# Four-layer sequence block: another order in the head of a first-phase step, two table calls on ScalarE, and the residual sum moved from GpSimd to VectorE

## The chip, the cores and the metric

One core of one Trainium2 chip runs the whole program in one launch. The metric is the device time of that launch in microseconds, of which lower is better. All data are float32 unless a line says otherwise.

## The reference

Four blocks run in sequence on x of 4 sequences, 1024 rows, 128 features. After each one, x becomes layernorm(x + block(x)).

- **Block 1, mixer and MLP.** `u = rmsnorm(x)`; `u @ in_proj` gives z (256 wide), xBC (512 wide) and 4 step sizes. xBC goes through a causal depthwise convolution of 4 taps with bias and then silu; the step sizes go through softplus. A state scan over the rows (4 heads of 64, 128 states) gives y, which is gated with silu(z), normalised, and projected back to 128; the result is added to x and called x1 below. Then `h = rmsnorm(x1)` and `mlp = (silu(h @ gate) * (h @ up)) @ down` with a hidden width of 512. The block returns x1 + mlp.
- **Block 2, expert layer.** 8 experts, a softmax gate, the best 2 of them weighted and summed.
- **Block 3, attention.** Layernorm, 16 heads of 8, full softmax over 1024 keys with a relative position bias, and an output projection.
- **Block 4, routed experts.** 8 experts of capacity 512, the best 2, with gather and scatter.

The change lies in block 1 and in what runs beside it. The residual sum x + x1, to which mlp is added before the layernorm, is one of its items.

## The kernel before

The kernel has three phases: a first phase (blocks 1 and 2 and the inputs of attention), attention, and the routed experts with the output. Every engine has its own program, written out by hand as a sequence of instructions, and the engines meet only through semaphores. An instruction waits in order, so whatever is queued behind a waiting instruction on its engine waits too.

**The first phase is software-pipelined over the four sequences.** The list `SLOTS` has six steps (m, p, q): m is the sequence whose mixer runs, p the one whose MLP and expert layer run, q the one whose attention inputs are made. Steps 1, 2 and 3 have an m and a p, steps 2 to 4 a p and a q; step 0 has only m = 0, step 5 only q = 3. Each step has a **head** and then a loop over 8 chunks of 128 rows. In the profiled execution the heads of steps 1, 2 and 3 begin near 121, 253 and 409 us, step 4 near 558 us, and attention near 664 us.

**The head.** For m: the step sizes (`step_sizes`), 12 input projections (`project`, one 128x128 weight by 512 rows each, in two passes), of which 4 are z and 8 go through the convolution. ScalarE copies each projection out of PSUM (`evac_projection`) and, for a convolved tile, makes the first tap with the bias (`tap`). VectorE adds the other three taps (`convolve`, L1782, three instructions of 128x512). ScalarE applies silu (`silu_conv`). For p: `rms_apply` (L1859) scales x1 by its inverse root into `x1n`, TensorE turns it (`rows_turned_mlp`), ScalarE copies it to `xnT` (`evac_T`, L1091). Then come eight steps n of the MLP: TensorE multiplies with `w_gate` and `w_up`, ScalarE makes silu of the first (`gate_silu`, L1179), VectorE multiplies both into `hidT` (`hidden`, L1867). After that TensorE runs `down` for the two halves of the rows, and VectorE adds each half to the residual sum `xa` (`skip_sum`, L1872). For q: `expert_norm` normalises a half of block 2's sum (L1699) and takes its statistics (L1681, L1686), and `tail_norm` applies attention's own layernorm (L1699).

**What ties the MLP's steps together.** The matmuls rotate through PSUM banks 5, 6 and 7, so on TensorE the gate product of step n waits for the product on VectorE of step n - 2:

```python
                if n >= 2:
                    pe.wait_ge(S.hid_ready, 2 * HID_TILES * b + n - 1)
                mm(bank(mlp_bank(2 * n)), tile(w_gate, f), xnT[:, half(H)])
```

TensorE's order in the loop is gate n, up n, projection 4 + n of the next mixer. `down` for half H waits for 7 + H products of `hidden`. VectorE's order before the change is `step_sizes`, convolution 0, both `rms_apply`, convolution 1, both halves of `expert_norm`, convolutions 2 and 3, and only then `hidden` 0.

**GpSimd** computes inverse roots (L1422), the two products `aU` of the first chunks (L1451), and, in the head, the residual sum `xa = xin + x1` (`skip_rows`, L1473). SyncE loads the input tile of sequence p + 2 after that sum (`res_sum`), and the stores of attention rows (`store_rows`) are queued behind that load.

ScalarE's function tables are loaded where the program changes between Exp and Silu. Copy, Identity and Square run with either of them. The load stands as ACT_TABLE_LOAD in the trace and carries the line of the activation that follows it.

Of the kernel before, what the change touches and what calls it, by code (L numbers as in the profile page):

```python
# [19 lines left out]
ALU = mybir.AluOpType  # L20
# [89 lines left out]
def build(nc, t):  # L110

    with ExitStack() as ctx:  # L112
        def sb(name, shape, dt=F32):
            return ctx.enter_context(nc.sbuf_tensor(name, shape, dt))
# [119 lines left out]
        rstd_mix = sb("rstd_mix", [P, NT])  # L234
        ss = sb("ss", [P, NT])
        rstd3 = sb("rstd3", [P, NT])

        o_rec = sb("o_rec", [P, HT, QUAD])
        smax = sb("smax", [P, 2, 16])
# [820 lines left out]
        def _(act):  # L1060
# [24 lines left out]
            def evac_T(kind, b, banks, **affine):  # L1085

                xnT_free(kind, b)
                for H in range(2):
                    act.wait_ge(S.xT_psum, turned(kind, b) + H + 1)
                    func = ACT.Identity if affine else ACT.Copy  # L1090
                    nc.scalar.activation(xnT[:, half(H)], bank(banks[H]), func, **affine).then_inc(S.xnT_ready, 1)  # L1091
# [18 lines left out]
            def evac_input(b):  # L1110
# [3 lines left out]
                for H, at in enumerate((TRB, SEGB)):  # L1114
                    act.wait_ge(S.in_T_psum, 2 * b + H + 1)
                    nc.scalar.activation(xinT[:, half(H)], bank(at), ACT.Copy).then_inc(S.in_T, 1)

            def step_exp(b):
                act.wait_ge(S.dt_abs, b + 1)
                nc.scalar.activation(dtu[:], dts[:], ACT.Exp, scale=-1.0).then_inc(S.dt_u, 1)  # L1120
# [94 lines left out]
            for m, p, q in SLOTS:  # L1215
                if m is not None:
                    evac_input(m)
                    step_exp(m)
                if p is not None:
                    mixed_squares(p, 1)  # L1220
                if m is not None:
                    for i in range(4):
                        evac_projection(m, i)
                        tap(m, i)
                if p is not None:
                    evac_T("mlp", p, (5, 6))
                for n in range(2 * HID_TILES):
                    if p is not None:
                        gate_silu(p, n)
                    if m is not None:  # L1230
                        evac_projection(m, 4 + n)
                        if 4 + n in CONVOLVED:
                            tap(m, CONVOLVED.index(4 + n))
                        if n >= 1:
                            silu_conv(m, n - 1)
                if m is not None:
                    silu_conv(m, N_CONV - 1)
                    decays(m)
                    chunk_copy(m, 0)
                if q is not None:  # L1240
                    act.wait_ge(S.w_late, LATE_LOADED)
                    act.wait_ge(S.late_ready, N_LATE)
                    evac_T("tail", q, (7, 6), scale=ln_g[:], bias=ln_b[:])
                if m is not None:
                    chunk_exp(m, 0, 0)
                    chunk_exp(m, 0, 1)
                if q is not None:
                    evac_queries(q)
                if m == 0:
                    act.wait_ge(S.w_late, LATE_LOADED)  # L1250
                    nc.scalar.activation(pick_rows[:].rearrange("k e n -> k (e n)"), pick_in, ACT.Copy).then_inc(S.late_ready, 1)
                for c in range(NT):
                    if m is not None and c < NT - 1:
                        chunk_copy(m, c + 1)
                        chunk_exp(m, c + 1, 0)
                    if p is not None and c == HT:
                        evac_gates(p)
                    if m is not None and c < NT - 1:
                        chunk_exp(m, c + 1, 1)
                    if m is not None and c in (2, 4, 6):  # L1260
                        gated_squares(m, c // 2 - 1)
                    if p is not None and c == 0:
                        evac_T("moe", p, (7, 5))
                    if p is not None and c == 2:
                        route_exp(p)
                    if q is not None and c < 3:
                        cut_part(q, c)
                    if m is not None and m + 1 < B and c == HT + 1:
                        input_squares(m + 1)
                if m is not None:  # L1270
                    gated_squares(m, HT - 1)
                    mixed_squares(m, 0)
# [104 lines left out]
        def _(pool):  # L1377
# [87 lines left out]
                                decay[:, 1, c].unsqueeze(2).to_broadcast([P, SSM_HEADS, SSM_DIM]),  # L1465
                                ALU.mult).then_inc(S.hdec_ready, 1)

            def skip_rows(b):

                pool.wait_ge(S.x1_ready, 2 * b + 2)  # L1470
                if b >= 1:
                    pool.wait_ge(S.normed, 6 * b - 4)
                g.tensor_tensor(xa[:], xin[:, b % 2], x1[:], ALU.add).then_inc(S.res_sum, 1)  # L1473

            input_root(0)
            g.memset(x3_all[:], 0.0).then_inc(S.zero_rows, 1)
            for m, p, q in SLOTS:
# [11 lines left out]
                    for H in range(2):  # L1489
                        norm_root(2, 6 * q + 4 + H, H)  # L1490
                if p is not None:
                    skip_rows(p)
                    for H in range(2):
                        norm_root(0, 6 * p + H, H)
                if m is not None:
# [126 lines left out]
        def _(dve):  # L1622
# [238 lines left out]
            def hidden(b, n):  # L1861
# [4 lines left out]
                    dve.wait_ge(S.q_part, 3 * (b - 1))  # L1866
                v.tensor_tensor(hidT[:, f, half(H)], silu_g[:, n % 2], bank(mlp_bank(2 * n + 1)), ALU.mult).then_inc(S.hid_ready, 1)  # L1867

            def skip_sum(b, H):
                dve.wait_ge(S.res_sum, b + 1)  # L1870
                dve.wait_ge(S.down_psum, 2 * b + H + 1)
                v.tensor_tensor(xa[:, own(H), :], xa[:, own(H), :], tiles4(5 + H), ALU.add).then_inc(S.skip_sum, 1)  # L1872
                dve.wait_ge(S.skip_sum, 2 * b + H + 1)
                statistics(xa, H, 0)
# [42 lines left out]
            def tail_norm(b, H):  # L1917
                if b >= 1:
                    dve.wait_ge(S.xT_psum, 2 * TURN_NO["tail", b - 1] + 2)
                normalise(kept(b), xn, H, 2, 6 * b + 4 + H)  # L1920
# [33 lines left out]
            for m, p, q in SLOTS:  # L1954
                if m is not None:
                    step_sizes(m)
                    convolve(m, 0)
                if p is not None:
                    for H in range(2):
                        rms_apply(p, H)  # L1960
                if m is not None:
                    convolve(m, 1)
                if q is not None:
                    for H in range(2):
                        expert_norm(q, H)
                if m is not None:
                    convolve(m, 2)
                for n in range(2 * HID_TILES):
                    if m is not None and n in (0, 3, 4, 5, 6):
                        convolve(m, 3 if n == 0 else n + 1)  # L1970
                    if p is not None:
                        hidden(p, n)
                    if q is not None and n == 2:
                        for H in range(2):
                            tail_norm(q, H)
                if p is not None:
                    for H in range(2):
                        skip_sum(p, H)
# [301 lines left out]
```

## Time and profile before

| what | value |
|---|---|
| median of 3 runs | 1643.79 us (1634.2, 1643.79, 1643.9) |
| the profiled execution | 1639.0 us, span 1637.3 us |
| mean granted TensorE clock | 0.904 |
| TensorE busy | 1378.8 us, 84% of the span |
| VectorE busy | 1116.4 us, 68% |
| ScalarE busy | 852.5 us, 52% |
| GpSimd busy | 314.6 us, 19% |

The span runs from the first to the last instruction. A granted clock of 1.00 is 2.4 GHz and 0.50 is 1.2 GHz. Busy shares are means over phases with different limits; attention alone is 876 us. In the rows below PE is TensorE's matmuls, DVE is VectorE, ACT is ScalarE and POOL is GpSimd, and L numbers are lines of the kernel.

### The profile page before, as it was taken

The numbers are of one execution on the slowest core, as the hardware profiler recorded it, in microseconds if no ns is written. First come the engines' busy times: TensorE is split into PE (matmuls) and PEld (weight loads), VectorE is DVE, ScalarE is ACT, GpSimd is POOL, SyncE is SP. The second block draws the span as 40 slices with busy tenths as digits, with TensorE's granted clock in tenths as the row PEclk, the third lists the DMA queues.
The fourth block names the chain that finished last, engine by engine and source line by source line (L and its number), as shares of the span: only waits on it lengthen the run. The fifth ranks groups of instructions, "written<-read, shape, count | busy, mean of one in ns | idle before, by whom it ended". The sixth has DMA issues, their size and how long they took to land. (4 is left out here: it accounts for less than half of the span.)

```text
span 1637.3 us, 20851 instructions
## 1 busy us (share of the span) xinstructions
PE 1378.8 (84%) x7344; PEld 615.8 (38%) x7344; DVE 1116.4 (68%) x2089; ACT 852.5 (52%) x1656; POOL 314.6 (19%) x444
## 2 busy tenths in 40 slices
PE   4778797889788877799999999999999999983560
PEld 2454473557355655122222333223332233322240
DVE  5647658565856555878888888888888888833115
ACT  5226214421532230277777777777777777772125
POOL 3221313122221301000000020141103211043351
PEclk9779998979889887589999999999999999996795
DMA  3070000020011247301111001111001100000224
GB/s 113 2 174 14 1 1 13 5 90 1 1 50 45 27 52 172 128 1 21 21 20 21 17 22 21 21 46 38 14 8 31 31 1 2 2 6 24 58 83 154
DMA packets 45965, 63.53 MB, mean 39 GB/s; under 512 B 8706, under 2 KB 33869, under 8 KB 44022
## 3 DMA queue, kind: packets, MB, share of 16 engines
q1 hardware_dynamic: 42790, 57.97, 14.6%
q0 software_dynamic: 3072, 4.23, 0.8%
q8 instruction: 59, 0.97, 0.3%
q14 instruction: 44, 0.36, 0.1%
HBM read 33.07 MB, written 31.15 MB: 39 GB/s over the span
## 5 line engine op out<-in xcount | busy, mean ns | idle before, releaser
L578 PE MATMUL ps<-space 128*32 128x512 f32 (+5 forms) x4608 | 860.3, 480 | 31.9 <-DVE smax L2048 7.6
L2048 DVE TENSOR_REDUCE smax<-ps 128x1 f32<-128x1024 f32 x512 | 605.2, 1220 | 116.1 <-PE ps L578 109.9
L1322 ACT ACTIVATE space<-ps 128x512 f32<-128x512 f32 x1024 | 555.5, 595 | 231.8 <-PE ps L578 231.1
L578 PEld LDWEIGHTS ps<-space 128*32 128x32 f32 (+5 forms) x4608 | 254.4, 110 | 614.2 <-ACT space L1322 329.2
L1420 POOL TENSOR_SCALAR eps_sum<-mv 128x4 f32<-128x4 f32 x32 | 7.3, 229 | 640.9 <-DVEq L1688 640.5
L578 PE MATMUL ps<-w_exp,space 128*128 128x128 f32 x512 | 86.2, 323 | 0.0
L1782 DVE SCALAR_TENSOR_TENSOR space<-space,conv_w 128x512 f32<-128x512 f32 x96 | 80.7, 850 | 4.2 <-ACT space L1151 1.6
L578 PEld LDWEIGHTS ps<-w_exp,space 128*128 128x128 f32 x512 | 74.1, 225 | 16.5 <-issue 16.5
L1198 ACT ACTIVATE btok<-ps 128x128 f32<-128x128 f32 x32 | 8.9, 277 | 135.1 <-DVE Gm L1800 68.8
L1530 POOL DMA_INDIRECT expert_in<-space,slot x64 | 62.9, 982 | 37.6 <-issue 19.3
L1902 DVE TENSOR_TENSOR space<-xnT,ps 128x512 f32<-128x512 f32 x64 | 42.1, 683 | 31.0 <-PE ps L578 31.0
L1204 ACT ACTIVATE space<-ps 128x512 f32<-128x512 f32 x64 | 38.1, 595 | 43.9 <-PE ps L578 43.8
L578 PE MATMUL ps<-space,w_in 128*128 128x512 f32 x96 | 54.7, 675 | 5.4 <-ACT space L1137 3.5
L571 PE MATMUL ps<-ident,space 128*128 128x128 f32 x192 | 32.6, 305 | 31.6 <-DVE space L1859 12.3
L578 PE MATMUL ps<-aU,ones 128*128 128x512 f32 x64 | 39.2, 697 | 22.9 <-ACT space L1204 22.6
L2203 DVE TENSOR_TENSOR space<-space,ps 96x512 f32<-96x512 f32 x16 | 10.9, 684 | 68.8 <-ACT space L1350 68.8
L578 PE MATMUL ps<-xnT,w_gate 128*128 128x512 f32 x64 | 39.5, 704 | 12.8 <-DVE space L1867 12.6
L1819 DVE TENSOR_TENSOR space<-space 128x512 f32<-128x512 f32 x32 | 28.7, 897 | 24.8 <-ACT space L1204 24.8
L1451 POOL TENSOR_TENSOR aU<-upto,av 128x512 f32<-128x512 f32 x32 | 36.9, 1157 | 41.4 <-PE ps L578 29.0
L1422 POOL TENSOR_TENSOR rstd<-eps_sum,neg_half 128x4 f32<-128x4 f32 x40 | 42.1, 1052 | 3.3
L1460 POOL TENSOR_TENSOR space<-space,decay 128x256 f32<-128x256 f32 x28 | 17.1, 612 | 120.5 <-issue 83.7
L571 PEld LDWEIGHTS ps<-ident,space 128*128 128x128 f32 x192 | 26.5, 158 | 36.3 <-issue 32.6
(246 smaller groups left out, 1457.3 us busy)
## 6 DMA issues: line engine op xcount, KB each, us to landing
q_rows<-space SPq DMA_DIRECT2D x24, 256.0 KB, 2.5
k_rows<-space SPq DMA_DIRECT2D x24, 256.0 KB, 2.8
space<-k_rows SPq DMA_DIRECT2D x16, 384.0 KB, 5.2
space<-q_rows SPq DMA_DIRECT2D x16, 384.0 KB, 6.8
expert_out<-x_all SPq DMA_DIRECT2D x2, 2048.0 KB, 20.4
space<-expert_out SPq DMA_DIRECT2D x4, 1024.0 KB, 8.8
v_rows<-space SPq DMA_DIRECT2D x4, 668.0 KB, 3.6
space<-v_rows SPq DMA_DIRECT2D x4, 668.0 KB, 6.5
```

The costliest lines, as they stand in the source:

```text
L571: last = nc.tensor.transpose(tile(dst, i), src(i), ident[:])
L578: return nc.tensor.matmul(out, lhsT, rhs, start=first, stop=last)
L1204: nc.scalar.activation(EL[:, c % 2, k].rearrange("p h n -> p (h n)"), bank(SEGB), ACT.Exp).then_inc(S.l_ready, 1)
L1322: nc.scalar.activation(prob[:, QUAD * (step % PROB_SETS) + unit % QUAD, :], bank(STB + unit % 2), ACT.Exp)\
L1422: g.tensor_tensor(out, eps_sum[:, 0:n], neg_half[:, 0:n], ALU.pow).then_inc(done, 1)
L1451: g.tensor_tensor(aU[:, c % 2], upto[:].unsqueeze(1).to_broadcast([P, SSM_HEADS, P]), av[:, c].unsqueeze(2).to_broadcast([P, SSM_HEADS, P] ...
L1460: g.tensor_tensor(xw[:, c % 2], xdt[:, c % 2], decay[:, 0, c].unsqueeze(2).to_broadcast([P, SSM_HEADS, SSM_DIM]), ALU.mult).then_inc(S.xw_ ...
L1530: g.indirect_dma_start(expert_in, bass.IndirectOffsetOnAxis(ap=slot[:, k, i:i + 1], axis=0), xrow[:, i, k, :], None, bounds_check=E * CAPA ...
L1782: ins = v.scalar_tensor_tensor(out, raw[:, f, lo + k:lo + k + HALF], conv_w[:, f, k:k + 1], out, ALU.mult, ALU.add)
L1819: v.tensor_tensor(Cs[:, c % 2], xbc[:, 3, c * P:(c + 1) * P].unsqueeze(1).to_broadcast([P, SSM_HEADS, P]), EL[:, c % 2, 1], ALU.mult).then ...
L1902: v.tensor_tensor(xs[:, k % XS_SLOTS], xnT[:, half(H)], bank(6 + k % 2), ALU.mult).then_inc(S.xs_ready, 1)
L2048: v.tensor_reduce(smax[:, N % 2, i:i + 1], ps[:, b0:b0 + 2, :].rearrange("p k n -> p (k n)"), AX.X, ALU.max).then_inc(S.s_max, 1)
```

## The change

- VectorE: both `rms_apply` come directly behind `step_sizes`; convolutions 0 and 1 follow. Convolutions 2 to 7 come one behind each of `hidden` 1 to 6. Where p and q both exist, the second half of `expert_norm` comes behind `hidden` 0, and `tail_norm` moves from behind step n = 2 to behind step n = 4.
- ScalarE: taps 2 and 3 come behind `evac_T`. A one-column Silu (`table_of`) stands ahead of `evac_T` where there is a p, and a one-column Exp behind the last `silu_conv` in every step.
- `skip_rows` leaves GpSimd and is done on VectorE behind the eighth `hidden`.

TensorE's and SyncE's programs are not edited.

```diff
@@ sb allocations
+        warm = sb("warm", [P, 2])
@@ ScalarE
+            def table_of(func, i):
+
+                nc.scalar.activation(warm[:, i:i + 1], neg_half[:, 0:1], func)
...
                 if m is not None:
-                    for i in range(4):
+                    for i in range(2):
                         evac_projection(m, i)
                         tap(m, i)
+                    for i in range(2, 4):
+                        evac_projection(m, i)
                 if p is not None:
+                    table_of(ACT.Silu, 0)
                     evac_T("mlp", p, (5, 6))
+                if m is not None:
+                    for i in range(2, 4):
+                        tap(m, i)
...
                 if m is not None:
                     silu_conv(m, N_CONV - 1)
+                table_of(ACT.Exp, 1)
+                if m is not None:
                     decays(m)
@@ GpSimd
-            def skip_rows(b):
-
-                pool.wait_ge(S.x1_ready, 2 * b + 2)
-                if b >= 1:
-                    pool.wait_ge(S.normed, 6 * b - 4)
-                g.tensor_tensor(xa[:], xin[:, b % 2], x1[:], ALU.add).then_inc(S.res_sum, 1)
...
-                    skip_rows(p)
@@ VectorE
+            def skip_rows(b):
+
+                if b >= 1:
+                    dve.wait_ge(S.normed, 6 * b - 4)
+                mine.wait(mine.n)
+                v.tensor_tensor(xa[:], xin[:, b % 2], x1[:], ALU.add).then_inc(S.res_sum, 1)
...
                 if m is not None:
                     step_sizes(m)
-                    convolve(m, 0)
                 if p is not None:
                     for H in range(2):
                         rms_apply(p, H)
                 if m is not None:
+                    convolve(m, 0)
                     convolve(m, 1)
                 if q is not None:
-                    for H in range(2):
-                        expert_norm(q, H)
-                if m is not None:
-                    convolve(m, 2)
+                    expert_norm(q, 0)
+                    if p is None:
+                        expert_norm(q, 1)
                 for n in range(2 * HID_TILES):
-                    if m is not None and n in (0, 3, 4, 5, 6):
-                        convolve(m, 3 if n == 0 else n + 1)
                     if p is not None:
                         hidden(p, n)
-                    if q is not None and n == 2:
+                    if q is not None and p is not None and n == 0:
+                        expert_norm(q, 1)
+                    if m is not None and 1 <= n <= N_CONV - 2:
+                        convolve(m, n + 1)
+                    if q is not None and n == 4:
                         for H in range(2):
                             tail_norm(q, H)
+                if p is not None:
+                    skip_rows(p)
                 if p is not None:
                     for H in range(2):
                         skip_sum(p, H)
```

## Rows read from the trace of the kernel before

**Rows 1.** Timeline of PE, step 2: start us, us, engine, line, what [idle before <-releaser].

```profile
263.72 1.91 PE L578 MATMUL ps<-xnT,w_gate 128*128 128x512 f32 x2 [0.19 <-ACT xnT L1091]
...
277.60 2.08 PE L578 MATMUL ps<-xnT,w_gate 128*128 128x512 f32 x2 [6.77 <-DVE space L1867]
...
295.59 7.38 PE L578 MATMUL ps<-w_down,space 128*128 128x128 f32 x64
```

**Rows 2.** Timeline of DVE, step 2.

```profile
257.99 3.63 DVE L1782 SCALAR_TENSOR_TENSOR space<-space,conv_w 128x512 f32<-128x512 f32 x3
261.54 1.28 DVE L1859 TENSOR_TENSOR space<-x,rstd 128x512 f32<-128x512 f32 x2
...
264.98 1.11 DVE L1699 TENSOR_SCALAR x_all<-x,mv,rstd 128x128 f32<-128x128 f32 x4
...
270.21 6.74 DVE L1782 SCALAR_TENSOR_TENSOR space<-space,conv_w 128x512 f32<-128x512 f32 x6
276.87 1.28 DVE L1867 TENSOR_TENSOR space<-space,ps 128x512 f32<-128x512 f32 x2
...
281.97 2.14 DVE L1699 TENSOR_SCALAR xn<-x_all,mv,rstd 128x128 f32<-128x128 f32 x8
284.02 2.32 DVE L1782 SCALAR_TENSOR_TENSOR space<-space,conv_w 128x512 f32<-128x512 f32 x3
286.26 0.68 DVE L1867 TENSOR_TENSOR space<-space,ps 128x512 f32<-128x512 f32 x1
286.86 2.32 DVE L1782 SCALAR_TENSOR_TENSOR space<-space,conv_w 128x512 f32<-128x512 f32 x3
...
299.50 0.69 DVE L1872 TENSOR_TENSOR xa<-xa,ps 128x512 f32<-128x512 f32 x1 [3.46 <-PE ps L578]
```

**Rows 3.** Timeline of POOL, step 2.

```profile
258.21 2.86 POOL L1451 TENSOR_TENSOR aU<-upto,av 128x512 f32<-128x512 f32 x2 [1.19 <-DVE av L1772]
...
271.83 2.33 POOL L1473 TENSOR_TENSOR xa<-xin,x 128x1024 f32<-128x1024 f32 x1
```

**Rows 4.** Timeline of ACT, step 2.

```profile
260.33 0.81 ACT L1151 ACTIVATE space<-space,conv_b,conv_w 128x512 f32<-128x512 f32 x1
...
264.19 1.28 ACT L1179 ACT_TABLE_LOAD   x1
265.67 0.60 ACT L1179 ACTIVATE space<-ps 128x512 f32<-128x512 f32 x1 [0.20 <-PE ps L578]
```

**Rows 5.** Windows of step 2: us, PE, PEld, DVE, ACT, POOL busy, PEclk, DMA, GB/s.

```profile
277.60:281.10 3.50, 3.50 (x5) 1.52 (x6) 0.55 (x1) 0.60 (x1) 0.00 (x0) 0.51 0.01 4
281.10:295.60 14.50, 14.42 (x34) 5.68 (x32) 13.95 (x26) 11.42 (x20) 0.00 (x0) 1.00 0.00 1
```

**Rows 6.** Timelines of ACT, PE and DVE, step 1.

```profile
128.07 0.81 ACT L1151 ACTIVATE space<-space,conv_b,conv_w 128x512 f32<-128x512 f32 x1
...
134.03 2.07 PE L578 MATMUL ps<-xnT,w_gate 128*128 128x512 f32 x2
...
140.47 0.69 DVE L1867 TENSOR_TENSOR space<-space,ps 128x512 f32<-128x512 f32 x1 [0.46 <-PE ps L578]
...
156.88 7.38 PE L578 MATMUL ps<-w_down,space 128*128 128x128 f32 x64
```

**Rows 7.** Timelines of DVE and PE, step 3.

```profile
413.69 3.64 DVE L1782 SCALAR_TENSOR_TENSOR space<-space,conv_w 128x512 f32<-128x512 f32 x3
...
451.56 7.38 PE L578 MATMUL ps<-w_down,space 128*128 128x128 f32 x64
```

**Rows 8.** Timeline of DVE, step 4.

```profile
569.35 0.69 DVE L1867 TENSOR_TENSOR space<-space,ps 128x512 f32<-128x512 f32 x1 [0.77 <-PE ps L578]
```

**Rows 9.** Timelines of PE behind the heads of steps 2 and 3.

```profile
308.16 1.97 PE L578 MATMUL ps<-aU,ones 128*128 128x512 f32 x2 [1.94 <-ACT space L1204]
...
464.13 1.12 PE L578 MATMUL ps<-aU,ones 128*128 128x512 f32 x2 [1.94 <-ACT space L1204]
```

**Rows 10.** Window of the attention phase.

```profile
664.00:1540.00 876.00, 814.39 (x4473) 246.73 (x4474) 675.23 (x918) 589.66 (x1087) 127.17 (x200) 0.95 0.10 23
```

## The prediction

> **What bounds the kernel now.** I read the page first: TensorE is busy 84% of the span, and about half of that is attention, which the change does not touch [rows 10]. So the change has to be read from the heads. I read the timelines of TensorE, VectorE, ScalarE and GpSimd over the head of step 2, then laid those of steps 1, 3 and 4 beside them.
>
> In step 2 TensorE begins the first gate product at 263.72, and its third gate product waits 6.77 us, until 277.60, for a product of VectorE [rows 1]. The releaser is `hidden` 0. Its two PSUM operands had been there for some ten us: VectorE did not reach it before 276.87, because two halves of `expert_norm` (264.98 to 270.21) and convolutions 2 and 3 stand ahead of it, and these last two were slowed [rows 2]. The wait costs twice, since TensorE comes back at half clock: 0.51 in the stretch after it, 1.00 in the one behind [rows 5], and the gate product's two passes take 2.08 us [rows 1], while 34 passes, 17 products, take 14.42 us at full clock [rows 5], 0.85 each. Later in the loop VectorE goes at 2.84 us a step (284.02 to 286.86: a convolution of 2.24 and a `hidden` of 0.60 by their starts [rows 2]) while TensorE has three products a step, 2.55 us. From there to `down` at 295.59 both keep nearly the same pace. What is to be seen is that VectorE has work for the whole head and does it in an order in which TensorE runs dry once. The limit after a reordering is VectorE's own sum of work.
>
> **The parts.** All sums are made against the profiled execution, 1639.0 us (span 1637.3, 1.7 around it), which is 4.8 under the median of the runs; these differ by 9.7 us among themselves.
>
> *VectorE's order, step 2.* VectorE is free at 257.99. Up to the end of `hidden` 6 the new order has: both scalings 1.2 (two in 1.28 [rows 2]), seven convolutions x 2.24 = 15.7, both halves of `expert_norm` 5.2 (264.98 to 270.21), `tail_norm` 2.05 (281.97 to 284.02), seven `hidden` x 0.60 = 4.2. Added to it is 1.3 us of blocking by GpSimd's two `aU` products: three instructions took 3.63 instead of 2.32 beside them [rows 2, 3]. The products do not go away, so I keep the 1.3, wherever it lands. What goes is the second blocking: six convolution instructions took 6.74 instead of 4.6 while `skip_rows` ran for 2.33 [rows 2, 3]. The sum is 29.7 us, `hidden` 6 ends at 287.7, and `down` can begin there at about 287.8 instead of 295.59 [rows 1]: 7.7 us gained, if VectorE is never kept waiting. `hidden` 7 ends 2.84 later, at 290.5, and the second half of `down` needs it only 3.7 us after the start of the first (7.38 for both).
>
> *Is VectorE kept waiting?* Its arrival at `hidden` 0 is 257.99 + 1.2 + 1.3 + 2 x 2.24 + 2.6 = 267.6. The first up product ends at most 3.8 us after the first gate starts (two of 1.91 at half clock [rows 1]), 265.6 if the gate starts at 261.8. It is not. Gate 2 needs `hidden` 0 (268.2) and TensorE has the six products of the first two steps done 7.2 us after the first gate (3.8 and four of 0.85), at 269.0: the 6.77 us wait is gone.
>
> *The start of the gate products.* `rms_apply` ends about 260.3 instead of 262.8, and ScalarE drops two taps of 0.8 ahead of the copy: tap 3 ended at 261.1 [rows 4], so the projections are copied by 259.5. Then the Silu load, 1.28, and the one-column call. No such call is in the trace; it lies between nothing and the 0.60 of the 128x512 activation [rows 4], and I take 0.2 because one column is nearer to nothing. With the copy of 0.6 the gate starts at about 261.7, against 263.72 [rows 1]. Taps 2 and 3 then run under the first gate product and are needed by VectorE only at 271.
>
> *What the Silu call is worth.* Before, the load ran under the first gate product: it ended at 265.47, and silu still waited 0.20 for TensorE [rows 4]. So the early call saves nothing there, and stands instead ahead of a copy on the path to TensorE; in steps 2 and 3 VectorE arrives later anyway and hides it. I cost it at nothing. The Trainium skill (ScalarE: Activation LUTs, What ACT_TABLE_LOAD costs) gives a switch 2.66 us in all, the load of 1.28 and a drain of 1.38. Here the load started directly behind the copy before it and its activation directly behind it where TensorE was done, which leaves no room for a drain. By the Trainium skill the first gate of step 1 would come 1.4 us later, and the sum below would be smaller by that.
>
> *Step 3* has the same rows: 413.69 + 29.7 + 0.1 = 443.5 against 451.56 [rows 7], 8.1 us gained.
>
> *Step 1* has no q, so TensorE bounds its start. Tap 3 ended at 128.9 [rows 6]; less 1.6, plus 1.28, 0.2 and 0.6, the gate starts at 129.5 instead of 134.03, 4.5 earlier. `hidden` 1 was bound by TensorE, 6.44 behind the gate (140.47 against 134.03 [rows 6]), so it ends at 136.5. Then VectorE has five convolutions and five `hidden` to the end of `hidden` 6, 5 x 2.84 = 14.2: 150.8. `down` starts at 151.0 instead of 156.88 [rows 6], 5.9 gained.
>
> *Step 4* has no m. `hidden` 1 started at 569.35 [rows 8], and now comes behind half an `expert_norm`; the gate product that needs it was due at 570.8 and would wait until 571. I take 0.3 lost, between 0 and 0.6; `tail_norm` only moves two steps on. The Exp call there saves a load that stood ahead of work for which VectorE was not waiting: nothing.
>
> *`skip_rows` on VectorE.* 1.3 us (two halves of 128x512 took 1.28 [rows 2]). It is queued ahead of `skip_sum`, which waited 3.46 us for `down` in step 2 [rows 2]. As `hidden` 7 now ends 2.8 behind `hidden` 6, not 0.6, the cover shrinks to about 291.7 - 290.5 = 1.2 us: just hidden, bounds 0 to 0.3. Without the cover it costs 1.3 a step. SyncE's input load waits for this sum, some 18 us later than now, and the stores queued behind it are due only in the chunk loop; the input tile is read about 80 us later. Nothing.
>
> *TensorE's clock.* This is the term that the trace does not fix. With `tail_norm` between steps 4 and 5 TensorE runs dry for 2.3 us ahead of its last three products. If the clock falls there they take twice 0.85 each: 2.6 more, of which some 2.2 reach `down`. Before, the same product of `aU` behind the same idle of 1.94 us took 1.97 us in step 2 and 1.12 in step 3 [rows 9]: such a gap brings half clock in one case of two. I take half, 1.1 in each of steps 2 and 3; the bounds are 0 and, with `down` beginning at half clock too, 3.9. The Trainium skill (TensorE: Matmul & The Clock Gate, Part 1) advises to leave the ramp out as under 1% of a typical span. Its term is 2.2 us here; without it the forecast would be 1618. The rows after the wait show that it has a price at this size [rows 5].
>
> **Sum:** 5.9 + 7.7 + 8.1 - 0.3 - 2.2 = 19.2 us. 1639.0 - 19.2 = 1619.8, so 1620. Everything behind `down` (decay sums, chunk loop, attention) hangs on it through TensorE and moves with it.
>
> **Rivals.**
>
> *A smaller gain.* VectorE is fully packed, so each hand-off that arrives late adds up, and the clock falls in every head. Price: 3.9 in steps 2 and 3, a half-clock `down` of 1.7 in step 1, 1.3 for an uncovered `skip_rows` in three steps: 7.8 + 1.7 + 3.9 = 13.4, of which 2.2 are in my sum. Gain 8.0, time 1631. For it: the cover of 1.2 is thin. Against: VectorE had 13.95 of 14.50 us busy before [rows 5] without losing its pace.
>
> *No change.* The head ends earlier and the time is given back behind it, in a wait that does not move (a transfer, a root on GpSimd). Time 1639. Against: `down` follows TensorE's own products with no idle row, and `skip_sum` waits for nothing but TensorE. For: attention is 876 us at clock 0.95 [rows 10], and 0.02 of clock there would be 18 us, as large as the gain.
>
> *Slower: the clock stays at half through the MLP loop.* In the new loop TensorE stops for a moment in each step instead of once for long. If that keeps the clock at 1.2 GHz, the 24 products of a loop take 24 x 1.7 = 41 us from the first gate: `down` at 302.7 in step 2 (7.1 later than before), 6.7 later in step 3, 13.6 in step 1. Sum +27, time 1666. It decides from a mean of 1.4 us a product on (295.59 - 261.7 = 33.9 for 24). Against: TensorE worked 2.55 of 2.84 us a step before, at 1.00 [rows 5], and that pace stays.
>
> *The calls do nothing.* If the load is not placed at the call, the gate starts 1.5 earlier, silu later, and VectorE's sum still decides: within 1 us of the forecast and part of it.
>
> **Numbers.** Forecast 0.69 (gains from 12 to 24), smaller gain 0.15, no change 0.10, slower 0.06. With the clock term at its lower bound and step 1 at full clock the gain is 21.4 + 1.8 = 23, 1616; with the upper one it is 13, 1626; the runs stand from 4.8 below to 4.9 above the profiled one. The range is 1611 to 1634, which leaves out the last two rivals and a little of the first. A change below 1% (16.4 us, to 1627.4) could not be told from none. The forecast lies above that with nine parts in ten, and the smaller gain with three: 0.69 x 0.93 + 0.15 x 0.3 = 0.69 faster; slower 0.06; the same 0.25.
>
> **What would show it.** Right: no idle of several us at the third gate of steps 2 and 3; `down` there about 30 us behind the end of `step_sizes` instead of 37.7; VectorE without a gap from the scalings to `hidden` 7; no convolution instruction of 2.9 us; the first gate of step 1 some 4.5 us earlier in its head. Wrong: VectorE waiting for TensorE in the loop, TensorE at 0.50 over the loop, `skip_sum` starting behind `skip_rows` by more than 0.3, or attention longer by more than a few us.

## The result and the profile after

The kernel after takes 1612.56 us where the kernel before takes 1639.31. The head of each step is shorter, and attention starts earlier by about as much.

| | before | after |
|---|---|---|
| median of 4 runs each | 1639.31 us | 1612.56 us (1609.37 to 1617.73) |
| ratio, 95% interval | | 0.9852 [0.9822, 0.9883] |
| span of the profiled execution | 1637.3 us | 1612.9 us |
| start of `av` (last of `step_sizes`) to start of `down`, steps 1, 2, 3 | 31.27, 37.71, 37.98 us | 24.71, 30.35, 30.77 us |
| start of the first scaling of x1 to start of `down`, step 4 | 19.70 us | 19.82 us |
| attention begins at | 664.07 us | 639.73 us |

A ratio here is the kernel's time by that of the kernel before, run beside it, with a 95% interval. This one is a gain of 24 us, or 19 to 29 by its interval. Of the 24.3 us by which attention starts earlier in the profile, the heads give 6.56 + 7.36 + 7.21 - 0.12 = 21.0; the other 3.3 lie outside the heads. Attention itself is as long as before, at the same clock [rows 10] (us, then busy us and instructions of PE, PEld, DVE, ACT and POOL, granted clock, DMA share, GB/s):

```profile
639.00:1516.00 877.00, 814.99 (x4474) 247.05 (x4475) 675.74 (x920) 589.82 (x1087) 127.58 (x200) 0.95 0.10 24
```

VectorE in step 2 after the change, from the end of `step_sizes` to both `skip_sum`, answers to [rows 2]:

```profile
253.33 0.19 DVE L1777 TENSOR_TENSOR av<-dt,a_neg 128x32 f32<-128x32 f32 x1
253.44 2.13 DVE L1864 TENSOR_TENSOR space<-x,rstd 128x512 f32<-128x512 f32 x2
255.49 5.33 DVE L1787 SCALAR_TENSOR_TENSOR space<-space,conv_w 128x512 f32<-128x512 f32 x6
260.74 1.11 DVE L1704 TENSOR_SCALAR x_all<-x,mv,rstd 128x128 f32<-128x128 f32 x4
...
263.38 0.69 DVE L1872 TENSOR_TENSOR space<-space,ps 128x512 f32<-128x512 f32 x1 [0.21 <-DVE mv L1691]
263.99 1.11 DVE L1704 TENSOR_SCALAR x_all<-x,mv,rstd 128x128 f32<-128x128 f32 x4
...
266.63 0.69 DVE L1872 TENSOR_TENSOR space<-space,ps 128x512 f32<-128x512 f32 x1 [0.21 <-DVE mv L1691]
267.24 2.32 DVE L1787 SCALAR_TENSOR_TENSOR space<-space,conv_w 128x512 f32<-128x512 f32 x3
...
277.97 2.14 DVE L1704 TENSOR_SCALAR xn<-x_all,mv,rstd 128x128 f32<-128x128 f32 x8
280.02 0.68 DVE L1872 TENSOR_TENSOR space<-space,ps 128x512 f32<-128x512 f32 x1
280.62 2.32 DVE L1787 SCALAR_TENSOR_TENSOR space<-space,conv_w 128x512 f32<-128x512 f32 x3
282.86 0.68 DVE L1872 TENSOR_TENSOR space<-space,ps 128x512 f32<-128x512 f32 x1
283.46 2.32 DVE L1787 SCALAR_TENSOR_TENSOR space<-space,conv_w 128x512 f32<-128x512 f32 x3
285.69 0.68 DVE L1872 TENSOR_TENSOR space<-space,ps 128x512 f32<-128x512 f32 x1
286.29 1.22 DVE L1879 TENSOR_TENSOR xa<-xin,x 128x1024 f32<-128x1024 f32 x1
287.60 0.69 DVE L1884 TENSOR_TENSOR xa<-xa,ps 128x512 f32<-128x512 f32 x1
```

From 253.44 to the end of `hidden` 6 at 283.54 VectorE stands still twice, for 0.21 us each time. Every convolution inside the MLP loop takes 2.32. The two scalings took 2.13 instead of 1.28, and the six convolution instructions behind them 5.33 instead of 4.56 (what six take in sum_only, undisturbed): that is the blocking by `aU`, 1.6 us in all, which has moved with GpSimd's row:

```profile
253.66 2.80 POOL L1464 TENSOR_TENSOR aU<-upto,av 128x512 f32<-128x512 f32 x2 [1.18 <-DVE av L1777]
```

`skip_rows` is the row of 1.22, and `skip_sum` follows it at once. TensorE beside it, against [rows 1]:

```profile
255.62 0.66 PE L572 MATMUL ps<-ident,space 128*128 128x128 f32 x4 [0.77 <-DVE space L1864]
257.00 1.12 PE L579 MATMUL ps<-xnT,w_gate 128*128 128x512 f32 x2 [0.72 <-ACT xnT L1092]
257.97 1.02 PE L579 MATMUL ps<-xnT,w_up 128*128 128x512 f32 x2
...
264.13 1.12 PE L579 MATMUL ps<-xnT,w_gate 128*128 128x512 f32 x2 [1.71 <-DVE space L1872]
...
267.37 1.12 PE L579 MATMUL ps<-xnT,w_gate 128*128 128x512 f32 x2 [0.41 <-DVE space L1872]
...
280.76 1.13 PE L579 MATMUL ps<-xnT,w_gate 128*128 128x512 f32 x2 [2.04 <-DVE space L1872]
281.72 1.02 PE L579 MATMUL ps<-xnT,w_up 128*128 128x512 f32 x2
282.58 1.02 PE L579 MATMUL ps<-space,w_in 128*128 128x512 f32 x2
283.68 7.38 PE L579 MATMUL ps<-w_down,space 128*128 128x128 f32 x64
```

The wait of 6.77 us at the third gate is 1.71 now. The gap behind `tail_norm` is there, 2.04, and no gate product takes 1.9 or more. The windows with these two gaps, and the stretch behind the second, were granted full clock throughout:

```profile
262.20:264.10 1.90, 0.22 (x1) 0.00 (x0) 1.65 (x9) 1.11 (x2) 0.70 (x2) 1.00 0.00 0
278.50:280.80 2.30, 0.26 (x2) 0.04 (x1) 2.30 (x9) 1.12 (x2) 0.00 (x0) 1.00 0.00 0
281.10:283.60 2.50, 2.50 (x6) 0.76 (x4) 2.43 (x5) 0.60 (x1) 0.00 (x0) 1.00 0.00 0
```

In step 1 GpSimd's `skip_rows` used to run beside the scalings of x1, 129.03 to 131.56, and VectorE in the kernel before needed 3.42 us for the two:

```profile
129.28 3.42 DVE L1859 TENSOR_TENSOR space<-x,rstd 128x512 f32<-128x512 f32 x2
```

Now they end sooner, and TensorE begins the first gate, against 134.03 [rows 6], at:

```profile
130.57 1.12 PE L579 MATMUL ps<-xnT,w_gate 128*128 128x512 f32 x2 [1.04 <-ACT xnT L1092]
```

From there to `down` (window, columns as above) it has no idle moment, 20.70 of 20.70 us busy, and VectorE has:

```profile
130.60:151.30 20.70, 20.70 (x49) 9.22 (x50) 19.28 (x29) 16.35 (x28) 0.00 (x0) 1.00 0.00 1
```

`skip_sum` of step 1 on VectorE waits 0.70 us for the end of `down`'s first half:

```profile
155.12 0.69 DVE L1884 TENSOR_TENSOR xa<-xa,ps 128x512 f32<-128x512 f32 x1 [0.70 <-PE ps L579]
```

### The profile page after: what moved, and what is told of

It is laid out like the page before. It is cut to its first block and busy times, and to the rows that moved or that the text cites. A ratio compares the mean times of both kernels' runs of the same rounds, so it can differ in the third digit from the quotient of the medians.

```text
span 1612.9 us, 20861 instructions
## 1 busy us (share of the span) xinstructions
PE 1368.9 (85%) x7344; PEld 610.7 (38%) x7344; DVE 1114.2 (69%) x2093; ACT 854.0 (53%) x1666; POOL 304.9 (19%) x440
## 5 line engine op out<-in xcount | busy, mean ns | idle before, releaser
L579 PE MATMUL ps<-w_exp,space 128*128 128x128 f32 x512 | 82.7, 314 | 0.0
L1787 DVE SCALAR_TENSOR_TENSOR space<-space,conv_w 128x512 f32<-128x512 f32 x96 | 74.8, 788 | 2.3
L1535 POOL DMA_INDIRECT expert_in<-space,slot x64 | 63.0, 984 | 37.6 <-issue 19.3
L579 PE MATMUL ps<-aU,ones 128*128 128x512 f32 x64 | 39.2, 697 | 22.9 <-ACT space L1209 22.8
L572 PE MATMUL ps<-ident,space 128*128 128x128 f32 x192 | 31.3, 293 | 20.7 <-DVE space L1754 11.2
L579 PE MATMUL ps<-xnT,w_gate 128*128 128x512 f32 x64 | 35.3, 634 | 12.1 <-DVE space L1872 9.4
L1802 DVE TENSOR_TENSOR space<-ps,dt 128x256 f32<-128x256 f32 x32 | 13.4, 420 | 38.9 <-PE ps L579 38.1
```

The lines of the kernel that those rows point to most:

```text
L572: last = nc.tensor.transpose(tile(dst, i), src(i), ident[:])
L579: return nc.tensor.matmul(out, lhsT, rhs, start=first, stop=last)
L1535: g.indirect_dma_start(expert_in, bass.IndirectOffsetOnAxis(ap=slot[:, k, i:i + 1], axis=0), xrow[:, i, k, :], None, bounds_check=E * CAPA ...
L1787: ins = v.scalar_tensor_tensor(out, raw[:, f, lo + k:lo + k + HALF], conv_w[:, f, k:k + 1], out, ALU.mult, ALU.add)
```

## Experiments

Times of steps below are from `av` to `down` unless said otherwise. The first four kernels ran on a chip on which the kernel before takes 1673.53 us, the others on chips where it takes 1638.67 and 1637.52, so whole times are compared within a group only. Single profiles of one kernel agree within 0.4 us in the heads of steps 1 to 3, but differ by some us outside them (after_again shows it).

**order_only.** The kernel before, with nothing but VectorE's new order (the hunks of the change for it, `skip_rows` left on GpSimd):

```diff
-                    convolve(m, 0)
                 if p is not None:
                     for H in range(2):
                         rms_apply(p, H)
                 if m is not None:
+                    convolve(m, 0)
                     convolve(m, 1)
...
+                    if q is not None and p is not None and n == 0:
+                        expert_norm(q, 1)
+                    if m is not None and 1 <= n <= N_CONV - 2:
+                        convolve(m, n + 1)
-                    if q is not None and n == 2:
+                    if q is not None and n == 4:
```

> Only VectorE's new order; the residual sum stays on GpSimd, ScalarE is as before. Theory 1 (the new order removes the 6.8 us wait of the third gate product, and VectorE's own work then sets the start of down): from the end of the step sizes to down, steps 2 and 3 take about 32.4 us (30.3 of the changed kernel and 2.1 for a convolution blocked by the sum on GpSimd) instead of 37.7 and 38.0, step 1 26.8 instead of 31.3; gain 15 us, 1624. Rival (the gain is the end of the blocking by GpSimd): steps 2 and 3 stay near 36 us, gain under 6.

Measured: 25.67, 32.38 and 32.42 us, and 1661.3 us, ratio 0.9921 [0.9895, 0.9947], 13 us. The order gives 5.6, 5.3 and 5.6 a step. What is missing against the full change in steps 2 and 3 (2.0 and 1.7) shows in one row of VectorE, the first convolution in the loop of step 2:

```profile
268.03 4.34 DVE L1782 SCALAR_TENSOR_TENSOR space<-space,conv_w 128x512 f32<-128x512 f32 x3
```

and in the one of GpSimd beside it:

```profile
268.68 2.35 POOL L1473 TENSOR_TENSOR xa<-xin,x 128x1024 f32<-128x1024 f32 x1
```

The same three instructions take 2.32 where `skip_rows` does not run: VectorE lost 2.02 us to an instruction of 2.35 us that began beside them. TensorE then stands idle in the loop for 2.10 us in step 2 and 2.08 in step 3, and in both the clock falls: at the gate product in step 3, at the up product behind it in step 2.

```profile
273.11 1.10 PE L578 MATMUL ps<-xnT,w_gate 128*128 128x512 f32 x2 [2.10 <-DVE space L1867]
274.05 1.79 PE L578 MATMUL ps<-xnT,w_up 128*128 128x512 f32 x2
...
420.91 2.02 PE L578 MATMUL ps<-xnT,w_gate 128*128 128x512 f32 x2 [2.08 <-DVE space L1867]
```

On the blocking: the Trainium skill (SBUF — State Buffer, SBUF: two separate sides) has a port pair that VectorE with two SBUF inputs and GpSimd hold in turn, each for its whole instruction; the 2.02 of 2.35 us agree.

**sum_only.** The kernel before, with `skip_rows` on VectorE ahead of `skip_sum`:

```diff
...
@@ GpSimd
-                    skip_rows(p)
@@ VectorE
+                if p is not None:
+                    skip_rows(p)
                 if p is not None:
                     for H in range(2):
                         skip_sum(p, H)
```

> Only the residual sum on VectorE; order and ScalarE as before. Theory 1: VectorE reaches the first product 2.1 us sooner in steps 2 and 3, and the scaling of step 1 is 2.1 us sooner; each head gains 2, in all 6 us, 1633, and the wait at the third gate stays at 4.6 us. Rival (the blocking is the main cost): 12 us or more. Third possibility (the wait ends with something else): nothing.

Measured: 28.33, 36.13 and 36.11, that is 2.94, 1.58 and 1.87 us sooner, and ratio 0.9964 [0.994, 0.9988], 6 us. (Step 4 is 0.36 shorter too, but it is so in tables_only as well, which leaves this sum alone.) The removed blocking is worth what was expected in total: 6.4 us in the three heads. The wait at the third gate of step 2 shrinks from 6.77 by 2.18 us, and the product still takes 2.08 (TensorE):

```profile
275.77 2.08 PE L578 MATMUL ps<-xnT,w_gate 128*128 128x512 f32 x2 [4.59 <-DVE space L1859]
```

Both parts alone sum to 16.5 + 6.4 = 22.9 us in steps 1 to 3, against 21.1 in the full change. In steps 2 and 3 the parts add up (6.9 and 7.4 against 7.36 and 7.21); in step 1 they give 8.5 against 6.56, since TensorE bounds that step from its first gate on, and order_only alone already starts the gate as early (3.8 us behind `av`, against 4.0).

**tables_only.** The kernel before, with both table calls, and the taps where they were:

```diff
                 if p is not None:
+                    table_of(ACT.Silu, 0)
                     evac_T("mlp", p, (5, 6))
...
                     silu_conv(m, N_CONV - 1)
+                table_of(ACT.Exp, 1)
+                if m is not None:
```

> Only the two calls that load function tables ahead, everything else as before. Theory 1: no effect, within 1 us, as the load ran under the first gate product. Rival (each early load takes 1.28 us off a head): 4 to 5 us faster. If the load holds back the copy of xnT: up to 1.5 us slower per head, 4 us in all.

Measured: 30.38, 38.42, 37.54, and ratio 1.0007 [0.9981, 1.0032]. The calls do what they say: the load stands at the call. No gain is to be seen, and one of over 3 us is excluded by the interval, which rules out the rival of 4 to 5 us. ScalarE in step 2 of this kernel:

```profile
264.89 1.28 ACT L1121 ACT_TABLE_LOAD   x1
266.18 0.20 ACT L1121 ACTIVATE warm<-neg_half 128x1 f32<-128x1 f32 x1
266.79 1.25 ACT L1092 ACTIVATE xnT<-ps 128x512 f32<-128x512 f32 x2 [0.41 <-PE ps L572]
```

The load and the call end before the copy's operand is there, and the copy still waits 0.41 us.

**tail_late.** The kernel after, with `tail_norm` behind the eighth `hidden` in steps 2 and 3, so that no `hidden` waits for it:

```diff
-                    if q is not None and n == 4:
+                    if q is not None and n == (4 if m is None or p is None else 7):
```

> The changed kernel with tail_norm behind the eighth hidden in steps 2 and 3 instead of behind the fifth. Theory 1: VectorE's work ahead of down is 2.05 us shorter, down starts 2 us sooner in both steps, the second half of the residual sum is late by 0.5; gain 3 us on the changed kernel, about 1610. Rival (TensorE's own products bound the loop): down does not move, and the late skip_sum makes it 1 to 4 us slower.

Measured: 28.30 and 28.72 instead of 30.35 and 30.77, 2.05 sooner in both, exactly the length of `tail_norm`. The head is VectorE's sum. The first copy of the decay products of the first chunk (`Gm`), which also needs VectorE, gains only 1.4 (39.0 and 39.4 us behind `av`, against 40.4 and 40.8), because both `skip_sum` now come behind `tail_norm`. The full change did not run on this chip, so 1647.38 us (0.9833 [0.98, 0.9866]) ranks it only against the kernel before, and the 3 us expected over the change are not tested by whole times.

**after_again, conv_ahead, conv_first, late_nosilu** ran on one chip. The first is the full change once more.

> The changed kernel as it is, for comparison on one chip. From the end of the step sizes to down: 24.7, 30.4 and 30.8 us in steps 1, 2 and 3, as in its first profile, since VectorE's work sets them and not chance in the clock; 21 us of gain from the heads, and 0 to 4 us more or less outside them.

Measured: 24.39, 30.38, 30.78; 1617.57 us, ratio 0.9856 [0.9829, 0.9882]. The heads repeat within 0.03 in steps 2 and 3. What lies outside them does not. From `down` of step 1 to `av` of step 2 it is 104.7 here (granted clock 0.90) and 102.1 in the first profile (0.92), with the same instructions; the kernel before had 101.0 (0.93), but tables_only, with VectorE's old order and the old sum, 104.3, so the change is not shown to lengthen it. From `down` of step 3 to the scaling of step 4 it is 108.1 here, 105.2 in the first profile and 108.5 before. Step 4's own stretch is 20.24, not 19.82. Single profiles differ by some us outside the heads, and part of it goes with the clock that TensorE was granted there.

**conv_ahead.** Convolution n + 2 behind `hidden` n, one step sooner, so that all eight are ahead of `hidden` 6:

```diff
-                    if m is not None and 1 <= n <= N_CONV - 2:
-                        convolve(m, n + 1)
+                    if m is not None and n <= N_CONV - 3:
+                        convolve(m, n + 2)
```

> The changed kernel with each of convolutions 2 to 7 one step earlier, behind hidden 0 to 5, so that convolution 7 stands ahead of hidden 6. VectorE's total work is the same. Theory 1 (down starts when VectorE has done what is queued up to hidden 6): down 2.24 us later in each of steps 1 to 3, 6.7 us slower than the changed kernel. Rival (only the wait at the third gate counted): within 1 us of the changed kernel.

Measured: 25.25, 33.06, 32.93: 2.68 and 2.15 later in steps 2 and 3, but 0.86 in step 1; 1623.13 us, 5.6 more than after_again. So keeping the eighth convolution behind `hidden` 6 is one full term of the gain in steps 2 and 3; in step 2 a fall of the clock, the gate of 1.97 below, comes on top. Step 1 has slack on VectorE, since TensorE bounds it. The idle rows of TensorE's loop in step 2 of this kernel:

```profile
267.46 1.13 PE L579 MATMUL ps<-xnT,w_gate 128*128 128x512 f32 x2 [1.74 <-DVE space L1872]
272.88 1.97 PE L579 MATMUL ps<-xnT,w_gate 128*128 128x512 f32 x2 [2.57 <-DVE space L1872]
286.80 1.12 PE L579 MATMUL ps<-xnT,w_gate 128*128 128x512 f32 x2 [1.66 <-DVE space L1872]
```

**conv_first.** Convolution 0 again ahead of both `rms_apply`:

```diff
                     step_sizes(m)
+                    convolve(m, 0)
                 if p is not None:
                     for H in range(2):
                         rms_apply(p, H)
                 if m is not None:
-                    convolve(m, 0)
                     convolve(m, 1)
```

> The changed kernel with convolution 0 ahead of the scaling of x1, as before the change. Theory 1: in steps 2 and 3 down does not move, as VectorE has the same work up to it and arrives at hidden 0 later than TensorE; in step 1 the first gate is 2.3 us later and up to 1.4 of it reaches down. In all 1 to 2 us slower than the changed kernel. Rival (the early scaling is what gains): 2.3 us in each of three heads, 7 slower.

Measured: 26.51, 30.05, 30.87, against 24.39, 30.38, 30.78. The early gate is worth 2.1 us in step 1 and nothing in steps 2 and 3, as the sum of VectorE says, though step 1 lost 0.7 more than the bound. The medians differ by 6.5 us, more than the expected 1 to 2; the intervals (0.9873 to 0.9919 here) overlap, and what the heads do not show of it stays open. The gate stands behind a longer idle of TensorE here. In step 1 it takes 1.13 us behind an idle of 3.17, in step 2 2.07 behind one of 3.41:

```profile
131.32 1.17 PE L572 MATMUL ps<-ident,space 128*128 128x128 f32 x8 [3.17 <-DVE space L1864]
132.63 1.13 PE L579 MATMUL ps<-xnT,w_gate 128*128 128x512 f32 x2
...
261.88 1.21 PE L572 MATMUL ps<-ident,space 128*128 128x128 f32 x8 [3.41 <-issue]
263.27 2.07 PE L579 MATMUL ps<-xnT,w_gate 128*128 128x512 f32 x2 [0.18 <-ACT xnT L1092]
```

**late_nosilu.** tail_late, and no Silu call:

```diff
                 if p is not None:
-                    table_of(ACT.Silu, 0)
                     evac_T("mlp", p, (5, 6))
```

> tail_norm behind the eighth hidden in steps 2 and 3 (as in tail_late), and without the Silu call ahead of the copy of xnT; the load then stands under the first gate product as before. Theory 1: down at 28.3 and 28.7 us behind the step sizes in steps 2 and 3, as with the call; in step 1 the first gate 1.3 us sooner and down up to 0.9 sooner. 3 to 4 us faster than the changed kernel. Rival (the call is what starts the gates early): first gate later in every head, down of step 1 up to 1.3 us later.

Measured: 24.22, 28.32, 28.72; 1612.82 us, ratio 0.9847 [0.9824, 0.987], 4.8 below after_again with overlapping intervals. Against tail_late the heads of steps 2 and 3 are unchanged, so the Silu call is worth nothing there, neither way. In step 1 the load only changes its place: the gate starts 0.9 sooner (2.78 behind `av` instead of 3.69), and gives 0.17 to `down`, because the load now stands behind both taps and the second up product waits for it. Step 2 shows the same hand-off on TensorE:

```profile
254.72 1.02 PE L579 MATMUL ps<-xnT,w_gate 128*128 128x512 f32 x2
...
258.89 1.12 PE L579 MATMUL ps<-xnT,w_up 128*128 128x512 f32 x2 [0.56 <-ACT space L1184]
```

and on ScalarE, where the load follows the taps:

```profile
255.42 1.51 ACT L1156 ACTIVATE space<-space,conv_b,conv_w 128x512 f32<-128x512 f32 x2
256.94 1.28 ACT L1184 ACT_TABLE_LOAD   x1
258.24 0.60 ACT L1184 ACTIVATE space<-ps 128x512 f32<-128x512 f32 x1
```

**after_third, combined** ran on one chip. The first is the full change again; the second is late_nosilu with taps 2 and 3 behind the first silu of the MLP, and `skip_sum` cut in two so that the inputs of the first chunk are taken ahead of the statistics of the second half:

```diff
@@ ScalarE
-                if m is not None:
-                    for i in range(2, 4):
-                        tap(m, i)
...
+                    if m is not None and n == 0:
+                        for i in range(2, 4):
+                            tap(m, i)
@@ VectorE
+            def skip_statistics(b, H):
...
-                    for H in range(2):
-                        skip_sum(p, H)
+                    skip_sum(p, 0)
+                    skip_statistics(p, 0)
+                    skip_sum(p, 1)
                 if m is not None:
                     chunk_inputs(m, 0)
+                if p is not None:
+                    skip_statistics(p, 1)
```

> The changed kernel again, beside the version below on one chip. Heads of 24.7, 30.4 and 30.8 us from the step sizes to down within 0.4 us; outside the heads it may differ by several us from profile to profile.

> The changed kernel with tail_norm behind the eighth hidden in steps 2 and 3, no Silu call, taps 2 and 3 behind the first gate silu, and the statistics of the second half of the residual sum behind the first chunk's inputs. Theory 1: down 28.3 and 28.7 us behind the step sizes in steps 2 and 3, 23.5 in step 1, where TensorE is then without a gap from its first gate on; the first chunk's inputs come 0.7 to 1.3 us closer behind down. In all 5 to 7 us faster than the changed kernel. Rival (what is taken from the head comes back in the chunk loop, as the statistics and the norm are late there): within 1 us of the changed kernel although down starts sooner.

Measured, after_third: 24.40, 30.36, 30.77; 1619.75 us, 0.9886 [0.9852, 0.992]. Measured, combined: 23.70, 28.30, 28.72, and `Gm` 32.9, 37.6 and 38.0 us behind `av`, against 34.4, 40.4 and 40.8 in after_third; 1604.24 us, 0.9801 [0.9773, 0.9829]. It beats both kernels: its interval lies below that of after_third, which ran beside it. In its step 2 TensorE begins `down` at:

```profile
285.19 3.03 PE L579 MATMUL ps<-w_down,space 128*128 128x128 f32 x25
```

and VectorE does, from the second `skip_sum`:

```profile
293.32 0.69 DVE L1883 TENSOR_TENSOR xa<-xa,ps 128x512 f32<-128x512 f32 x1 [0.21 <-DVE mv L1690]
294.13 0.42 DVE L1801 TENSOR_TENSOR space<-ps,dt 128x256 f32<-128x256 f32 x1
294.47 0.28 DVE L1804 TENSOR_TENSOR Gm<-ps,upto 128x128 f32<-128x128 f32 x1
```

`Gm` stands 9.28 us behind the start of `down`, with no statistics between it and the second `skip_sum`; in the change it is 10.06 (293.74 against 283.68). The heads explain 7.1 us at `Gm` (1.5 + 2.8 + 2.8); the medians differ by 15.5, and the two profiled executions by 4.2. So the size of the gain is open: the runs of combined stand in two groups, 1601.7 to 1604.3 (four) and 1612.8 to 1614.4 (two), with the profile in the upper one, while those of after_third are 1618.6 to 1625.7 but for one of 1608.8. What parts the groups no run shows.

## Why the prediction held, step by step

The forecast of 19.2 us gave 1620; the profiles differ by 24.4 us and the medians by 26.8, so 1612.56 lies in the range of 1611 to 1634, but near its lower end. The mechanism was right: order_only, tail_late and conv_ahead each move `down` by what they move in VectorE's sum. The clock term, the bound of step 1 and some sizes were not. From 19.2 to the 24.3 of the profile it is 2.2 (clock), 0.7 (step 1), -0.3 and -0.9 (steps 2 and 3), 0.2 (step 4), and 3.3 from outside the heads.

- **VectorE's sum in steps 2 and 3: right.** The prediction had 29.7 us from the first scaling to the end of `hidden` 6; step 2 took 30.1. Most of the 0.4 is the blocking by `aU`, 1.6 instead of 1.3. The two idle moments of 0.21 us, behind the statistics, are not: the 5.2 for both halves of `expert_norm` came from rows that held such pauses already, and they take 5.28 now. In step 3 the second pause is 0.60, and the sum 30.5; that and `aU` are most of what 7.21 lacks of 8.1. Why that pause is longer stays open. tail_late takes 2.05 out of the sum and `down` comes 2.05 sooner, conv_ahead adds 2.24 and it comes 2.68 and 2.15 later: the sum sets `down`.
- **Both blockings: right in kind.** The one by `aU` stayed and moved, and grew by 0.3. The one by `skip_rows` is 2.02 in the row of order_only and was to be 2.14. That it also held up the scalings of step 1, 3.42 us instead of 1.28, the prediction did not see; sum_only, which takes only it away, starts the first gate there 2.6 us sooner.
- **Cover of `skip_rows`: right, just hidden.** `skip_sum` starts at 287.60 with no idle and no lateness: `down`'s first half began at 283.68, and in step 1, where it can be seen, `skip_sum` waits 0.70 us.
- **Step 1: the size held (6.56 against 5.9) for the wrong reason.** The prediction let VectorE bound the step and put the gate 4.5 sooner. The gate came 4.4 sooner (4.0 behind `av` instead of 8.42), but VectorE was not the bound: TensorE has no idle from there on. Its first product ran at full clock, so that all 24 take 20.7 us, while VectorE ended `hidden` 6 at 150.5, 0.8 ahead of `down`. That the two errors, clock and bound, left the size nearly right is luck. conv_ahead, with 2.24 more on VectorE, costs 0.86 there.
- **First gate in step 2: the start held, its clock did not.** It was to be 2.0 sooner; relative to `av` it is 3.67 instead of 5.84, 2.2. It takes 1.12 us instead of 1.91, with idles of only 0.77 and 0.72 us ahead of it, where the kernel before stood idle for 3.45; the prediction had kept half clock there. It changes nothing in steps 2 and 3, where VectorE bounds.
- **TensorE's clock, -2.2: the term that failed.** The gap was sized well (2.04 us against 2.3). The fall did not come in either step; the same gap of step 3, 2.04 us, also has a gate of 1.13 behind it, and after_again and after_third have four more gaps of 2.04 and 2.05 with 1.12 and 1.13. So for this kernel the bound of 0 was the right end. The length of the gap does not say so: behind 2.10 and 2.08 in order_only the clock fell both times. What parts the cases stays open. The Trainium skill (TensorE: Matmul & The Clock Gate, Part 1) would have left the term out; in this gap that was right, while sum_only still pays it behind an idle of 4.59.
- **Step 4: -0.12 against -0.3, and not measured that well.** The product expected to wait waits 0.68, but full clock came sooner ahead of it (up product 1.41 instead of 1.91, gate 1.02 instead of 1.38), which covers the wait. The change takes 20.24 and 20.21 in after_again and after_third, 0.5 more than the kernel before.
- **The Silu call: right, nothing.** The one-column call takes 0.20 us, as assumed. The Trainium skill's drain (ScalarE: Activation LUTs, What ACT_TABLE_LOAD costs) does not show: in tables_only the call starts 0.01 us behind the load of 1.28, and in late_nosilu the first silu 0.02 behind it. The first gate of step 1 starts 4.0 us behind `av`, where the sum had 3.9 and the drain would have made it 5.3.
- **Outside the heads, 3.3 us: not in the sum, and luck.** The same instructions run there. after_again and after_third repeat the heads within 0.03 in steps 2 and 3, but their attention begins at 645.2, not 639.7: 18.8 us earlier than before, where their heads give 20.9. The 3.3 us are the shorter stretch behind step 3, which neither repeats. So 3.3 is within what two profiles of one kernel differ by, and no part of the change is shown to cause it. Whole times say the same: the two repeats gave ratios of 0.9856 and 0.9886, gains of 24 and 19 us, so how near 1620 the forecast came is not known to better than some us.

The rivals: a clock at half through the loop did not occur (from the first gate to `down` it is 0.86 us a product in step 1 and 1.11 in step 2, under the 1.4 named as the mark). Time given back behind `down` is not to be seen in the first profile; in the repeats attention starts 2 us less early than the heads give, within the scatter. The smaller gain needed an uncovered `skip_rows` and the clock's fall; neither is in the rows.

## What to carry to other kernels

Where one engine feeds another through a short ring of buffers, first add up all that stands ahead of the product that ends the stage on the feeding engine; what isn't needed for it goes behind it, and each such move gives about its full length (2.05 us for one of 2.05, 2.15 and 2.68 for one of 2.24) only where that engine bounds, so check each stage for its own bound. An addition on GpSimd beside VectorE instructions with two operands in SBUF cost VectorE nearly its whole length here, and is dearer there than on VectorE itself (2.0 us against 1.2) where the latter has a wait to hide it in. Loading a function table ahead of its use gave nothing here, where the load already ran beside a product of TensorE; no run has a load that holds up the activation behind it for its whole length.

## What the runs showed of the hardware

- Behind idles of 1.40 to 1.90 us in the MLP loop TensorE's gate took 1.12 to 1.13 us, as at full clock, and behind 4.59 and more it took 2.07 or 2.08. Between these it went either way: 1.12 and 1.13 behind all six idles of 2.04 and 2.05 in three profiles of the change, a fall behind 2.08 and 2.10 in order_only; 1.97 behind 2.57 and 1.13 behind 2.93 in conv_ahead; 1.12 behind 2.70 in combined; 1.13 with an idle of 3.17 ahead and 2.07 with one of 3.41 in two heads of conv_first. Before, an idle of 1.94 us had come out both ways behind the heads [rows 9]. The idle just ahead alone does not tell it.
- The kernel before took 1638.7 and 1637.5 us on two chips and 1673.5 on a third, 2% more. Each kernel has to be compared with one that ran beside it.
